# Attention scores of a decoder layer: two heads as two 64-row products instead of one product with block-diagonal keys

## The chip, the cores and the metric

The kernel runs on one core of one Trainium2 chip. The metric is the device time of one execution in microseconds (us); lower is better. All inputs lie in the chip's main memory at the start, and the output is stored there.

## The reference, cut to what matters

The reference is a decoder layer on four sequences of 256 tokens of width 512, with a layer norm after each of three parts. The change touches the second part, attention to 64 context positions with 32 query heads that share 8 key and value heads:

```python
x = _layernorm(x + _L0_attn_ref(x, ...))                  # x @ masked (w1.T w2.T), gelu
x = _layernorm(x + _L0_xattn_ref(x, ctx, ctx, mask, wq, wk, wv, wo, 0))
x = _layernorm(x + _L0_ffn_ref(x, ...))                   # dense + routed low-rank part
# in _L0_xattn_ref:
q = (query @ wq).reshape(bs, sq, HQ, DK).transpose(0, 2, 1, 3)    # HQ = 32, DK = 128, sq = 256
k = (key @ wk).reshape(bs, sk, HKV, DK)                           # HKV = 8, sk = 64
v = (value @ wv).reshape(bs, sk, HKV, DV)
...                                                               # each k, v head serves 4 query heads
q = apply_rope(q, pos)
k = apply_rope(k, ...)
scores = jnp.einsum('bhqd,bhkd->bhqk', q, k) / scale
attn = jax.nn.softmax(scores + m[:, None, :, :], axis=-1)
out = jnp.einsum('bhqk,bhkd->bhqd', attn, v)
return out.transpose(0, 2, 1, 3).reshape(bs, sq, HQ * DV) @ wo
```

## The kernel before, in words

The 1024 tokens are 8 tiles (`t`) of 128, two tiles to a sequence. Attention goes in 8 groups (`g`), one for each key/value head, with its 4 query heads. Groups 1 to 6 are a hardware loop (`Fori(1, LAST)`, `LAST` is 7); group 0 and group 7 are written out around it. Nothing is scheduled while it runs: every engine has its own list of steps in an order written out by hand, and the engines keep step by counting semaphores (`wait_ge`). An engine never passes a step that waits.

Most large products are made of three products of a rounded 32-bit type, high and low parts, by `mm3` (L255 to L257): the high part times the high part, and the two mixed ones. ScalarE (ACT) makes the high part by a copy (L763), and VectorE (DVE) or GpSimd (POOL) the low part by a subtraction (L1102 on VectorE). The steps of one group on TensorE (PE) are:

- `keys(g)`, `values(g)`: keys and values of the group's head.
- `query(g, u, f)`, 8 times: queries of a unit. A unit `u` (4 in a group, `UNITS`) is two heads (`a` = 0, 1) times 512 tokens. `f` is 0 or 1 for the first or second 64 of the 128 dimensions of a head, as the rotary embedding pairs them. So in `QR[:, u % 2, f, tokens]` the partitions 0 to 63 hold dimensions of one head and 64 to 127 the same dimensions of the other.
- `scores(g, u)` (L348): plain 32-bit products. For each of 4 token tiles and both `f` the stationary operand is `QR` (128 partitions by 128 tokens) and the moving one is `KBD`, 128 by 128, the keys written block-diagonally: head 0's 64 rows go with columns 0 to 63, head 1's with columns 64 to 127, and zeros stand elsewhere. So one product gives both heads' scores. One such product in 32 bits is two weight loads and two matmul instructions in the trace.
- VectorE then takes the scores in PSUM (`mask_scores` L1241, `row_max` L1246, `shift` L1253), ScalarE does the exponential (L860), VectorE the sums and inverses (L1258, L1262), GpSimd the scaling (`probs`, L1697).
- `probs_transpose(g, u)` (L355): the probabilities transposed, 4 tiles.
- `value_out(g, n, b)`: values times the output weights, 3 matmuls into bank `b`; high and low parts go to `VWh` and `VWl`.
- `attend(g, t)`: probabilities times `VW`, 6 matmuls; `accumulate` (L1280) adds the bank to the residual `X`.

The 8 PSUM banks are given out by hand: 0 and 1 for queries with `f` = 0, 2 for `f` = 1, 3 for `value_out`, 4 for scores, 5 for transposed probabilities, 6 and 7 for `attend` in turn. Behind group 7 each tile's statistics are taken on VectorE, GpSimd finds the inverse root by Newton steps (L1676 to L1682), ScalarE normalizes, and `x2_tile(t)` (L261) transposes the tile for the dense part (`base`, `lora_in`, `lora_out`). The product at L300, with one row (`PTh[0:1, ...]`), adds the bias in the first dense part, once in each of 8 tiles; L386, L421 and L426 are small products of the router.

Of the kernel before, what the change touches and what calls it, by code (L numbers as in the profile page):

```python
# [15 lines left out]
P = 128  # L16
# [15 lines left out]
def decoder_layer(nc, x, ctx_in, amask, w1, w2, b2, smask, wq, wk, wv, wo, fW, fb, fA, fB, rW, rb, rope, out):  # L32
# [24 lines left out]
    with ExitStack() as es:  # L57
# [18 lines left out]
        KBD = sb("KBD", [P, B, 2, P])  # L76
# [31 lines left out]
        QB_BANK, S_BANK, T_BANK, PV_BANK = 2, 4, 5, 6  # L108
# [4 lines left out]
        kbd_zero wq_hi wq_lo wo_hi wo_lo wkv_hi wkv_lo k_mm k_sw k_cos k_sin k_add k_rot v_mm v_hi v_lo  # L113
# [38 lines left out]
        def v_out(g):  # L152
            return bank[:, T_BANK if isinstance(g, int) and g == 0 else 1, 0:B * KS]
# [4 lines left out]
        def x2_bank(t):  # L158
            return (3, 5, 4, 4, 5, 3, 5, 3)[t]
# [14 lines left out]
        def by_head(ap, t):  # L174

            return ap.rearrange("p (a t k) -> p a t k", a=2, k=KS)[:, :, t, :]

        def fy_bank(t):
            return (0, 6, 2, 7, 1, 3, 2, 7)[t]
# [8 lines left out]
        F_BANKS = (1, 3, 3, 2, 2, 1, 1)  # L188
        LORA_BANKS, ROUTE_BANK = (4, 3), 5
# [62 lines left out]
        def _(pe):  # L252
# [87 lines left out]
            def scores(g, u):  # L340
# [26 lines left out]
            def attend(g, t):  # L367
# [5 lines left out]
                for pair in range(2):  # L373
                    m = mm3(bank[:, PV_BANK + t % 2, :], PTh[:, pair, t * P:(t + 1) * P], PTl[:, pair, t * P:(t + 1) * P],
# [114 lines left out]
            pe.wait_ge(sm["x_added"], 8)  # L489
            value_out(0, 0, 3)  # L490
# [4 lines left out]
            pe.wait_ge(sm["tr_lo"], 14)  # L495
# [3 lines left out]
            pe.wait_ge(sm["vw_lo"], n_vw(0, 0))  # L499
# [5 lines left out]
            pe.wait_ge(sm["vw_lo"], n_vw(0, 1))  # L505
            value_out(0, 2, 3)
            pe.wait_ge(sm["k_cos"], 1)
            scores(0, 0)
            pe.wait_ge(sm["q_rot"], n_rot(0, 0, 0))
            query(0, 2, 0)  # L510
            pe.wait_ge(sm["vw_lo"], n_vw(0, 2))
# [7 lines left out]
            pe.wait_ge(sm["v_lo"], 1)  # L519
# [3 lines left out]
            pe.wait_ge(sm["vw_lo"], n_vw(0, 3))  # L523
            value_out(0, 4, 3)
# [7 lines left out]
            value_out(0, 5, 3)  # L532
            pe.wait_ge(sm["tr_lo"], 17)
            attend(0, 0)
# [1329 lines left out]
```

## Time and profile before

| | before |
|---|---|
| median of 3 runs | 520.07 us (520.02 to 523.38) |
| the profiled execution, its own time | 519.7 us |
| its span on the core | 517.9 us |
| outside the span | 1.8 us |
| mean granted TensorE clock | 0.992 of full |
| TensorE matmul busy | 498.5 us, 96% of the span |
| TensorE weight load busy | 420.7 us |
| VectorE, ScalarE, GpSimd busy | 411.5, 259.6, 268.0 us |

The span is from the first to the last instruction that the profile shows. A matmul's row has the start at which it was taken up and a modelled end, so neighbours overlap; what a matmul costs in a stream is the distance from its start to the start of the next.

### The profile page before, as it was taken

The page shows a single profiled execution, that of the slowest core. Times are in us where ns is not written, and L with a number is a line of the kernel's source. Part 1 is how long each engine was busy: PE and PEld are TensorE (multiplying, and loading weights), DVE is VectorE, ACT ScalarE, POOL GpSimd, SP SyncE. Part 2 cuts the span into 40 slices and gives each one's busy share as a digit, 9 for nine tenths or more (in the row PEclk, how much of TensorE's full clock was granted, in tenths as well). Part 3 has the DMA queues.
Part 4 walks back from the last instruction along what each step waited for, and adds up shares of the span by engine and source line. Part 5 has one row for each costly group of instructions (what it writes and reads, how often), then busy time and mean ns, then how long its engine had stood idle before and what let it go on. Part 6 is the DMA issues. An engine that isn't in the chain of part 4 may idle for free.

```text
span 517.9 us, 7997 instructions
## 1 busy us (share of the span) xinstructions
PE 498.5 (96%) x2637; PEld 420.7 (81%) x2637; DVE 411.5 (79%) x742; ACT 259.6 (50%) x462; POOL 268.0 (52%) x344
## 2 busy tenths in 40 slices
PE   5999999999999999999999999999999999989992
PEld 4777788888888888888888888888888888868781
DVE  4557789887888778878887888788878869999475
ACT  4372375763465355635653574367346635363332
POOL 3173264873575358436742675276627632127724
PEclk9999999999999999999999999999999999989998
DMA  8942010122013002300230023002200230000004
GB/s 296 356 139 106 1 41 1 56 76 74 1 53 132 18 0 81 121 0 0 81 121 0 0 81 121 0 0 81 81 0 0 93 51 1 1 1 1 1 0 163
DMA packets 27596, 31.48 MB, mean 61 GB/s; under 512 B 6321, under 2 KB 14769, under 8 KB 27578
## 3 DMA queue, kind: packets, MB, share of 16 engines
q1 hardware_dynamic: 27578, 31.25, 18.9%
q8 instruction: 10, 0.16, 0.1%
q14 instruction: 8, 0.07, 0.0%
HBM read 29.15 MB, written 2.10 MB: 60 GB/s over the span
## 4 chain that ended last, share of the span: by engine, by line
PE 90%; DVE 2%; POOL 2%; DMA 2%; issue 1%; SPq 1%; ACT 1%; POOLq 0%; DVEq 0%
PE bank L255 24%; PE bank L257 24%; PE bank L256 24%; PE bank L348 11%; PE bank L355 3%; PE bank L261 2%; DMA CTX<-in_ctx_dram 2%; PE bank L300 1%; PE bank L388 1%; DVE VWl L1102 1%; POOL NW L1680 1%; POOL NW L1678 0%; POOL RS L1682 0%; POOL NW L1676 0%; DVE BST L1152 0%
## 5 line engine op out<-in xcount | busy, mean ns | idle before, releaser
L1691 POOL TENSOR_TENSOR QS<-QS,SIN 128x512 f32<-128x512 f32 x64 | 83.0, 1296 | 131.8 <-ACT QS L763 126.7
L1102 DVE TENSOR_TENSOR VWl<-bank,VWh 64x512 fp32r<-64x512 f32 (+1 forms) x132 | 90.9, 689 | 21.3 <-ACT VWh L763 19.4
L255 PE MATMUL bank<-XTh,WQh 128*128 128x512 f32 x256 | 102.3, 400 | 0.0
L763 ACT ACTIVATE VWh<-bank 64x512 fp32r<-64x512 f32 (+1 forms) x132 | 78.1, 592 | 45.4 <-PE bank L257 43.1
L257 PE MATMUL bank<-XTh,WQl 128*128 128x512 f32 x256 | 99.9, 390 | 0.0
L256 PE MATMUL bank<-XTl,WQh 128*128 128x512 f32 x256 | 99.8, 390 | 0.0
L763 ACT ACTIVATE QS<-bank 128x512 f32<-128x512 f32 x64 | 38.3, 599 | 112.7 <-PE bank L257 112.6
L348 PEld LDWEIGHTS bank<-KBD,QR 128*128 128x128 f32 x512 | 61.8, 191 | 2.3
L348 PE MATMUL bank<-KBD,QR 128*128 128x128 f32 x512 | 62.3, 275 | 0.0
L1216 DVE TENSOR_TENSOR bank<-bank,COS 128x512 f32<-128x512 f32 x64 | 44.6, 697 | 20.2 <-ACT QS L763 19.8
L1667 POOL TENSOR_TENSOR WOl<-WOr,WOh 128x512 fp32r<-128x512 f32 x32 | 41.1, 1288 | 31.9 <-ACT WOh L763 31.9
L257 PEld LDWEIGHTS bank<-XTh,WQl 128*128 128x128 f32 x256 | 48.0, 188 | 10.3
L256 PEld LDWEIGHTS bank<-XTl,WQh 128*128 128x128 f32 x256 | 48.2, 188 | 9.2
L255 PEld LDWEIGHTS bank<-XTh,WQh 128*128 128x128 f32 x256 | 48.2, 188 | 9.1
L255 PE MATMUL bank<-VWh,PTh 128*128 128x512 f32 x128 | 51.2, 400 | 0.0
L257 PE MATMUL bank<-VWh,PTl 128*128 128x512 f32 x128 | 50.1, 391 | 0.0
L256 PE MATMUL bank<-VWl,PTh 128*128 128x512 f32 x128 | 49.9, 390 | 0.0
L1226 DVE TENSOR_TENSOR QR<-bank,QS 128x512 f32<-128x512 f32 x64 | 43.2, 680 | 2.3 <-POOL QS L1691 2.1
L1280 DVE TENSOR_TENSOR X<-X,bank 128x512 f32<-128x512 f32 x64 | 42.8, 677 | 1.2 <-PE bank L257 0.6
L1657 POOL TENSOR_TENSOR WQl<-WQr,WQh 128x512 fp32r<-128x512 f32 x32 | 41.2, 1300 | 3.0 <-ACT WQh L763 3.0
L1697 POOL TENSOR_TENSOR SM<-SM,RI 128x512 f32<-128x512 f32 x32 | 33.5, 1048 | 13.2 <-DVE RI L1262 13.1
L255 PE MATMUL bank<-WOh,VTh 128*128 128x512 f32 x64 | 27.3, 427 | 2.3 <-DVE VWl L1102 2.2
(146 smaller groups left out, 953.7 us busy)
## 6 DMA issues: line engine op xcount, KB each, us to landing
WQr<-in_L_xattn_wq_dram SPq DMA_DIRECT2D x8, 1024.0 KB, 5.5
WOr<-in_L_xattn_wo_dram SPq DMA_DIRECT2D x8, 1024.0 KB, 5.4
KVr<-in_L_xattn_wk_dram SPq DMA_DIRECT2D x8, 256.0 KB, 3.8
KVr<-in_L_xattn_wv_dram SPq DMA_DIRECT2D x8, 256.0 KB, 4.1
out_dram<-X SPq DMA_DIRECT2D x8, 256.0 KB, 2.1
X<-in_x_dram SPq DMA_DIRECT2D x3, 512.0 KB, 9.4
WQr<-in_L_attn_w_dram SPq DMA_DIRECT2D x4, 256.0 KB, 3.4
WOr<-in_L_attn_w_dram SPq DMA_DIRECT2D x4, 256.0 KB, 4.8
```

Of the source, the lines that this page charges most:

```text
L255: pe.matmul(o, lh, rh, start=start, stop=False)
L256: pe.matmul(o, lh, rl, start=False, stop=False)
L257: return pe.matmul(o, ll, rh, start=False, stop=stop)
L348: m = pe.matmul(by_head(bank[:, S_BANK, :], t), QR[:, u % 2, f, t * P:(t + 1) * P], KBD[:, b, f, :].rearrange("p (a k) -> p a k", a=2), st ...
L763: return act.activation(o, i, ACT.Copy)
L1102: return dve.tensor_tensor(o, i, f32(hi), ALU.subtract)
L1216: dve.tensor_tensor(q, q, by_pos(COS, 2, S), ALU.mult).then_inc(sm["q_cos"], 1)
L1226: dve.tensor_tensor(QR[:, u % 2, f, :], bank[:, q_bank(u, f), :], QS[:, u % 2, 1 - f, :], ALU.add if f else ALU.subtract).then_inc(sm["q_r ...
L1280: dve.tensor_tensor(X[:, t, :], X[:, t, :], bank[:, PV_BANK + t % 2, :], ALU.add)\
L1657: pool.tensor_tensor(wq_split(WQl, h), wq_head(WQr, h), f32(wq_split(WQh, h)), ALU.subtract)\
L1667: pool.tensor_tensor(WOl[:, h, :], WOr[:, h, :], f32(WOh[:, h, :]), ALU.subtract)\
L1691: pool.tensor_tensor(q, q, SIN[:, :].unsqueeze(1).broadcast_to([P, 2, S]), ALU.mult)\
```

## The change: what it does

The keys are no longer written block-diagonally. `KK` holds them densely: partitions 0 to 63 and 64 to 127 each have the same 64 dimensions, 64 keys wide. `scores` issues, for each token tile and each `f`, two products of 64 rows: head 0's on partitions 0 to 63 and head 1's on 64 to 127, each 128 tokens stationary and 64 keys moving, into the same columns of two different PSUM banks (4 and 5). The 8 products of a unit become 16. Nothing is written in zeros any more (the memset on GpSimd and its semaphore are gone).

Since scores now hold two banks, the other banks are given out anew: transposed probabilities go to bank 7 or 5 by unit, `attend` to 7, 3, 7, 6, 3, 7, 6, 7 by tile, and `value_out` to 3, 6 or 7. The written-out orders of all four engines are other ones, with other waits; VectorE's and ScalarE's operations on scores have the same sizes over two banks.

```diff
-        KBD = sb("KBD", [P, B, 2, P])
+        KK = sb("KK", [P, B, 2, KS])
...
-        QB_BANK, S_BANK, T_BANK, PV_BANK = 2, 4, 5, 6
+        QB_BANK, S_BANK, PV_BANK = 2, 4, 6
+        T_BANKS, A_BANKS = (7, 7, 5, 7), (7, 3, 7, 6, 3, 7, 6, 7)
...
+        def s_all():
+            return bank[:, S_BANK:S_BANK + 2, 0:4 * KS]
...
                 for t in range(4):
                     b = 2 * (u // 2) + t // TPB
                     for f in range(2):
-                        m = pe.matmul(by_head(bank[:, S_BANK, :], t), QR[:, u % 2, f, t * P:(t + 1) * P],
-                                      KBD[:, b, f, :].rearrange("p (a k) -> p a k", a=2), start=f == 0, stop=f == 1)
+                        for a in range(2):
+                            head = slice(64 * a, 64 * a + 64)
+                            m = pe.matmul(bank[:, S_BANK + a, t * KS:(t + 1) * KS], QR[head, u % 2, f, t * P:(t + 1) * P],
+                                          KK[head, b, f, :], start=f == 0, stop=f == 1)
                 m.then_inc(sm["s_mm"], 1)
...
-                    m = pe.transpose(bank[:, T_BANK, t * P:(t + 1) * P], SM[:, u % 2, t * P:(t + 1) * P], ID[:, :])
+                    m = pe.transpose(bank[:, T_BANKS[u], t * P:(t + 1) * P], SM[:, u % 2, t * P:(t + 1) * P], ID[:, :])
...
-                    m = mm3(bank[:, PV_BANK + t % 2, :], PTh[:, pair, t * P:(t + 1) * P], PTl[:, pair, t * P:(t + 1) * P],
+                    m = mm3(bank[:, A_BANKS[t], :], PTh[:, pair, t * P:(t + 1) * P], PTl[:, pair, t * P:(t + 1) * P],
...
-                        m = copy(KBD[64 * a:64 * a + 64, :, f, KS * a:KS * a + KS],
+                        m = copy(KK[64 * a:64 * a + 64, :, f, :],
                                  KC[64 * f:64 * f + 64, :].rearrange("p (b k) -> p b k", b=B))
...
-            pool.memset(KBD[:, :, :, :], 0.0).then_inc(sm["kbd_zero"], 1)
```

The orders are shown at three places. The first is TensorE in the loop, around the scores of a unit 0: what stands there before.

```order
L255 MATMUL bank<-WOh,VTh 128x512 [waits v_lo,wo_lo]
L256 MATMUL bank<-WOl,VTh 128x512
L257 MATMUL bank<-WOh,VTl 128x512
L559 REGISTER_ALU
L342 ISA [waits s_sub]
L348 MATMUL bank<-KBD,QR 128x2x64 [waits k_rot,q_rot]
L348 MATMUL bank<-KBD,QR 128x2x64 x7
L330 REGISTER_ALU [waits v_lo]
L255 MATMUL bank<-XTh,WQh 128x512 [waits wq_lo]
```

And the same place in the changed kernel:

```order
L257 MATMUL bank<-XTh,WQl 128x512
L342 ISA [waits pt_lo,s_sub]
L350 MATMUL bank<-KK,QR 128x64 [waits k_rot,q_rot]
L350 MATMUL bank<-KK,QR 128x64 x15
L255 MATMUL bank<-WOh,VTh 128x512 [waits wo_lo,vw_lo]
L256 MATMUL bank<-WOl,VTh 128x512
```

8 products stand as 16, half as wide; the scores also wait for `pt_lo`, since their second bank, 5, is the one of unit 2's transposed probabilities; and the query of unit 1 stands ahead of them instead of behind.

The second place is TensorE behind group 7's scores: the last `value_out` steps (`WOh,VTh`), the last `probs_transpose` (`ID,SM`) and the first `x2_tile` (`ID,X`). Before:

```order
L255 MATMUL bank<-WOh,VTh 128x512 [waits vw_lo]
L256 MATMUL bank<-WOl,VTh 128x512
L257 MATMUL bank<-WOh,VTl 128x512
L355 MATMUL bank<-ID,SM 128x128 [waits p_done,pt_lo]
L355 MATMUL bank<-ID,SM 128x128 x3
L255 MATMUL bank<-WOh,VTh 128x512 [waits vw_lo]
L256 MATMUL bank<-WOl,VTh 128x512
L257 MATMUL bank<-WOh,VTl 128x512
L388 MATMUL bank<-ID,WOr 128x128 [waits fa_in,f_lo]
```

In the changed kernel:

```order
L390 MATMUL bank<-ID,WQr 128x128 [waits q_rot]
L390 MATMUL bank<-ID,WQr 128x128 x3
L357 MATMUL bank<-ID,SM 128x128 [waits p_done,x_added]
L357 MATMUL bank<-ID,SM 128x128 x3
L255 MATMUL bank<-VWh,PTh 128x512 [waits vw_lo]
...
L261 MATMUL bank<-ID,X 128x128 [waits ln_out,s_sub]
L261 MATMUL bank<-ID,X 128x128 x3
L261 MATMUL bank<-ID,X 128x128 [waits ln_out,pt_lo]
L261 MATMUL bank<-ID,X 128x128 x3
```

One `attend` (6 matmuls) stands now between the last `probs_transpose` and the first `x2_tile`; before, one `value_out`, two weight transposes and three `attend` did.

The third place is GpSimd's start. Before:

```order
L1735 MEMSET KSW 1x128
L1736 MEMSET KBD 128x1024
L1715 TENSOR_TENSOR WOl<-WOr,WOh 128x512 x2
L1662 TENSOR_TENSOR KVl<-KVr,KVh 128x512 x2
L1657 TENSOR_TENSOR WQl<-WQr,WQh 128x4x2x64 x2
```

In the changed kernel:

```order
L1736 ISA
L1736 AFFINE_SELECT ID<-ID 128x128
L1738 MEMSET KSW 1x128
L1718 TENSOR_TENSOR WOl<-WOr,WOh 128x512 x2
L1665 TENSOR_TENSOR KVl<-KVr,KVh 128x512 x2
```

One memset is gone, and nothing else moved there.

## Rows read from the trace of the kernel before

**Rows 1.** The page: busy time, and the chain that ended last, by engine and line.

```profile
PE 498.5 (96%) x2637; PEld 420.7 (81%) x2637; DVE 411.5 (79%) x742; ACT 259.6 (50%) x462; POOL 268.0 (52%) x344
...
PE bank L255 24%; PE bank L257 24%; PE bank L256 24%; PE bank L348 11%; PE bank L355 3%; PE bank L261 2%; DMA CTX<-in_ctx_dram 2%; PE bank L300 1%; PE bank L388 1%; DVE VWl L1102 1%; POOL NW L1680 1%; POOL NW L1678 0%; POOL RS L1682 0%; POOL NW L1676 0%; DVE BST L1152 0%
```

**Rows 2.** Busy time of each engine by stretch: one loop pass, and behind the last scores.

```profile
core 0: us, PE busy (x) PEld busy (x) DVE busy (x) ACT busy (x) POOL busy (x), PEclk, DMA share, GB/s
...
176.00:226.00 50.00, 50.00 (x273) 43.13 (x273) 41.18 (x67) 26.38 (x49) 28.23 (x24) 1.00 0.17 52
...
445.00:484.00 39.00, 35.90 (x179) 28.67 (x177) 34.30 (x76) 18.04 (x30) 17.87 (x62) 0.96 0.00 1
```

**Rows 3.** TensorE groups of the scores: 512 matmuls, and their 512 weight loads.

```profile
L348 PE MATMUL bank<-KBD,QR 128*128 128x128 f32 x512 | 62.3, 275 | 0.0
...
L348 PEld LDWEIGHTS bank<-KBD,QR 128*128 128x128 f32 x512 | 61.8, 191 | 2.3
```

**Rows 4.** TensorE in time (start, us): a score unit with transposes behind it.

```profile
204.93 0.39 PE L257 MATMUL bank<-XTh,WQl 128*128 128x512 f32 x1
205.16 1.95 PE L348 MATMUL bank<-KBD,QR 128*128 128x128 f32 x16
206.94 0.60 PE L355 MATMUL bank<-ID,SM 128*128 128x128 f32 x4
```

**Rows 5.** TensorE's weight loads in time, right behind them.

```profile
207.27 0.19 PEld L255 LDWEIGHTS bank<-WOh,VTh 128*128 128x128 f32 x1
207.38 0.19 PEld L256 LDWEIGHTS bank<-WOl,VTh 128*128 128x128 f32 x1
```

**Rows 6.** Matmuls in time around two products of one row, L300 and L301.

```profile
43.42 0.39 PE L257 MATMUL bank<-VWh,XTl 128*128 128x512 f32 x1
43.74 0.49 PE L300 MATMUL bank<-PTh 1*128 1x512 f32 x1
44.07 0.39 PE L301 MATMUL bank<-PTl,PTh 1*128 1x512 f32 x1
44.40 0.50 PE L255 MATMUL bank<-VWh,XTh 128*128 128x512 f32 x1
44.73 0.40 PE L256 MATMUL bank<-VWl,XTh 128*128 128x512 f32 x1
```

**Rows 7.** Weight loads at the same place.

```profile
43.74 0.18 PEld L300 LDWEIGHTS bank<-PTh 1*128 1x128 f32 x1 [0.35 <-issue]
43.84 0.18 PEld L301 LDWEIGHTS bank<-PTl,PTh 1*128 1x128 f32 x1
44.39 0.19 PEld L255 LDWEIGHTS bank<-VWh,XTh 128*128 128x128 f32 x1 [0.36 <-issue]
```

**Rows 8.** Matmuls in time around the router's 8 products with 4 stationary columns.

```profile
488.43 0.35 PE L421 MATMUL bank<-RWT,QT 128*4 128x8 f32 x8
488.71 0.50 PE L255 MATMUL bank<-XTh,WOh 128*128 128x512 f32 x1
```

**Rows 9.** TensorE in time behind the last scores: first and last of each wait.

```profile
455.15 0.40 PE L257 MATMUL bank<-WOh,VTl 128*128 128x512 f32 x1
457.16 0.50 PE L255 MATMUL bank<-WOh,VTh 128*128 128x512 f32 x1 [1.61 <-DVE VWl L1102]
...
459.13 0.79 PE L255 MATMUL bank<-WOh,VTh 128*128 128x512 f32 x1 [0.57 <-DVE VWl L1102]
459.72 0.63 PE L256 MATMUL bank<-WOl,VTh 128*128 128x512 f32 x1
460.15 0.63 PE L257 MATMUL bank<-WOh,VTl 128*128 128x512 f32 x1
460.58 1.78 PE L388 MATMUL bank<-ID,WOr 128*128 128x128 f32 x8
```

**Rows 10.** GpSimd in time at the start.

```profile
1.55 0.94 POOL L1736 MEMSET KBD<- 128x1024 f32 x1
8.88 1.28 POOL L1715 TENSOR_TENSOR WOl<-WOr,WOh 128x512 fp32r<-128x512 f32 x1 [6.39 <-ACT WOh L763]
```

More of the change, by code:

```diff
@@ L152, in v_out @@
         def v_out(g):
-            return bank[:, T_BANK if isinstance(g, int) and g == 0 else 1, 0:B * KS]
+            return bank[:, 5 if isinstance(g, int) and g == 0 else 1, 0:B * KS]
         def tr_bank(n):
@@ L590, in _ @@
                 query(g, 3, 0)
+                pe.wait_ge(sm["x_added"], n_added(g - 1, 7))
+                probs_transpose(g, 0)
+                pe.wait_ge(sm["x_added"], n_added(g - 1, 6))
+                value_out(g, 4, 6)
                 pe.wait_ge(sm["q_rot"], n_rot(g, 2, 0))
                 keys(g + 1)
+                pe.wait_ge(sm["q_rot"], n_rot(g, 2, 1))
+                query(g, 3, 1)
+                pe.wait_ge(sm["s_sub"], n_unit(g, 1))
+                scores(g, 2)
                 pe.wait_ge(sm["pt_lo"], n_unit(g, 0))
@@ L622, in _ @@
+            value_out(LAST - 1, 7, 3)
+            pe.wait_ge(sm["x_added"], n_added(LAST - 1, 0))
+            attend(LAST - 1, 2)
+            pe.wait_ge(sm["vw_lo"], n_vw(LAST - 1, 5))
+            attend(LAST - 1, 3)
+            pe.wait_ge(sm["s_sub"], n_unit(LAST - 1, 3))
+            probs_transpose(LAST - 1, 2)
             pe.wait_ge(sm["v_lo"], LAST + 1)
             query(LAST, 1, 0)
+            pe.wait_ge(sm["s_sub"], n_unit(LAST - 1, 3))
             pe.wait_ge(sm["pt_lo"], n_unit(LAST - 1, 2))
+            scores(LAST, 0)
@@ L637, in _ @@
             query(LAST, 2, 0)
[L638 to L641 removed]
+            pe.wait_ge(sm["pt_lo"], n_unit(LAST - 1, 3))
+            value_out(LAST, 1, 7)
+            pe.wait_ge(sm["vw_lo"], n_vw(LAST, 0))
+            attend(LAST - 1, 4)
+            pe.wait_ge(sm["s_sub"], n_unit(LAST, 0))
+            scores(LAST, 1)
             pe.wait_ge(sm["q_rot"], n_rot(LAST, 1, 1))
@@ L651, in _ @@
-            query(LAST, 3, 0)
-            pe.wait_ge(sm["vw_lo"], n_vw(LAST, 0))
-            weight_transpose(1)
+            pe.wait_ge(sm["q_rot"], n_rot(LAST, 2, 0))
+            weight_transpose(0)
+            pe.wait_ge(sm["x_added"], n_added(LAST - 1, 4))
+            value_out(LAST, 3, 3)
+            pe.wait_ge(sm["q_rot"], n_rot(LAST, 2, 1))
+            query(LAST, 3, 1)
+            pe.wait_ge(sm["pt_lo"], n_unit(LAST, 0))
+            attend(LAST - 1, 5)
+            pe.wait_ge(sm["vw_lo"], n_vw(LAST, 2))
@@ L694, in _ @@
+            probs_transpose(LAST, 3)
+            pe.wait_ge(sm["vw_lo"], n_vw(LAST, 7))
+            attend(LAST, 3)
+            pe.wait_ge(sm["s_sub"], n_unit(LAST, 3))
+            x2_tile(0)
+            pe.wait_ge(sm["pt_lo"], n_unit(LAST, 2))
+            x2_tile(1)
+            pe.wait_ge(sm["vw_lo"], n_vw(LAST, 6))
+            attend(LAST, 4)
+            pe.wait_ge(sm["pt_lo"], n_unit(LAST, 3))
+            attend(LAST, 5)
+            pe.wait_ge(sm["f_lo"], 1)
+            base(0)
             pe.wait_ge(sm["f_lo"], 4)
@@ L840, in k_spread @@
                 act.wait_ge(sm["k_add"], g + 1)
-                if isinstance(g, int) and g == 0:
-                    act.wait_ge(sm["kbd_zero"], 1)
-                else:
+                if not (isinstance(g, int) and g == 0):
                     act.wait_ge(sm["s_mm"], n_unit(g - 1, 3))
@@ L965, in _ @@
             k_swap(0)
[L966 removed]
+            vw_hi(0, 0, 7)
             wkv_hi(1)
@@ L1232, in s_rows @@
             def s_rows():
-                return bank[:, S_BANK, :].rearrange("p (r k) -> p r k", k=KS)
+                return s_all().rearrange("p a (t k) -> p a t k", k=KS)
             def mask_scores(g, u):
```

550 lines of the change are left out of this document (254 added, 296 removed).

## The prediction

> **What bounds the kernel now.** I read the page first, then the busy time by stretch, then TensorE in time. The chain that ended last is nine tenths TensorE, and the score products alone, L348, are 11% of it [rows 1]. In a loop pass TensorE is busy 50.00 of 50.00 us while VectorE, the next engine, is busy 41.18 [rows 2]. Of the 32 units of scores (8 groups times 4; the 512 matmuls are 32 times 16) 24 lie in the six passes and the others right around them. There every microsecond added to or taken from TensorE's work goes straight into the time, and nothing else does, as long as VectorE keeps its 8.8 us of slack. The new order can gain only behind the last scores, where TensorE waits.
>
> **What a unit of scores costs now.** The 16 matmuls of one unit start at 205.16, and what follows starts at 206.94: 1.78 us, 0.111 us for each pair of a weight load and a matmul [rows 4]. Thirty-two of them are 57 us, which is the 11%. The group rows give 275 ns for a matmul and 191 ns for a load [rows 3]; these overlap, so the spacing is the cost, not the duration. Which of the two sets the 0.111? The loads alone can be seen where long matmuls follow: the load at 207.27 is followed by the next at 207.38, 0.11 us later, although the matmul between them is 512 wide [rows 5]. So a load of 128 columns takes 0.11 us of the load path. The matmul has about the same length, or less, hidden behind it. Does a load of fewer rows cost less? The only loads of this kind with fewer rows are those with one row: 43.74 and 43.84, 0.10 us apart [rows 7]. Against 128 rows that is the same. Products of 64 rows lie between one and 128 rows, so I take 0.11 us for each of their loads.
>
> **The change, part by part.**
>
> Score products: a unit's 8 products of 128 rows and 128 moving columns become 16 of 64 rows and 64 columns. Each is still two loads and two matmuls, so 16 loads of 0.11 us become 32. The stationary side, 128 tokens, is as wide as before; only the moving side is halved. The matmul shrinks, at most 0.111 to an estimated 0.055 us by its columns, but the matmul hid behind the load anyway. What decides is whether head 0's loads (rows 0 to 63) and head 1's (rows 64 to 127) go side by side. No row of this trace shows two row halves at work, so I bound it. If they do not overlap, 32 loads are 3.52 us. If they do, the order of the program is A, A, B, B, A, A, B, B (A for head 0, two parts each); a head's next load can start when its last matmul has, the first step holds one load of A alone, and from then on each step of 0.11 us holds one of either head: 17 steps, 1.87 us. I take the second, since the two products share neither rows nor PSUM bank, and price the first as a rival.
>
> The Trainium skill ("TensorEngine Tiling (Array Packing)", Key Properties) says that different tiles can execute weight loads and matmuls in parallel. No run shown here tells; without it the choice stands on the disjoint rows alone.
>
> Changing the shape of the array: the trace shows what a product that doesn't use all the rows costs beside its own work. L300 and L301 use one row. From the matmul at 43.42 to the one at 44.73 are four steps, 1.31 us, where four steps of 0.23 (204.93 to 205.16 [rows 4]) would be 0.92: 0.39 us for going in and coming out [rows 6]. The loads tell why: the one at 43.74 and the one at 44.39 each come after an idle time of 0.35 us and are not pulled ahead of the matmul before them [rows 7]. The same shows at 488.43 to 488.71 with 4 columns: eight pairs in 0.28 us, where the next matmul comes late too [rows 8]. So each way costs 0.09 us until the first load may start (0.32 less 0.23), and then the load itself, 0.11, bare. A unit of 64-row products stands between full-height ones on both sides, so it pays this 32 times in and 32 times out. Bounds: nothing, if half the rows are no other shape, and 0.39 us as here. I take the upper, the only one that a row shows.
>
> The sum for one unit: 0.09 in, 17 steps of 0.11 = 1.87, the last matmul 0.055, 0.09 out, and 0.11 for the next load in the open: 2.22 us, against 1.78. That is 0.44 more, times 32 = **+14 us**.
>
> The Trainium skill (the same page and section) says that changing the tiling mode drains TensorE, and names no price; the trace agrees, with the 0.09 us each way.
>
> Keys: ScalarE's four copies have the same 64x256 size and only land elsewhere; zero. GpSimd's memset, 0.94 us, ends at 2.49 us, and GpSimd then idles 6.39 us for ScalarE [rows 10]: zero, and if that cover were gone, 0.94. VectorE's three operations on scores read two banks instead of one, with the same 512 elements in a row; zero for TensorE, because of the 8.8 us of slack.
>
> New banks and orders in the loop: the same steps, with other waits. New is that scores of unit 0 wait for unit 2's transposed probabilities, whose bank they need; behind that wait stand in TensorE's queue a `value_out` and the next query. A query stands ahead of them now, 12 matmuls of 0.23 us or 2.7 us, which covers the copy and the subtraction. TensorE waits nowhere in the loop before, so nothing can be gained (below: none); a wait of some tenths a pass would give at most 1 us times 8. I take zero, since a slower TensorE leaves all the others more time.
>
> Behind the last scores: TensorE waits 1.61 and 0.57 us for `VWl`, and then takes steps of 0.43 us (459.72 to 460.15) and eight transposes in 1.78 us, where four took 0.60 [rows 4, 9]: its clock is at the lower of its two levels, 1.2 instead of 2.4 GHz, and the granted clock of the whole stretch is 0.96 [rows 2]. The two waits are 2.2 us, the slow spell about one more (0.20 us for each of the three steps, less for the transposes). VectorE, 34.3 of 39 us busy [rows 2], would let a better order return no more than 4.7. The new order takes away the bank shared by neighbours in `value_out`, but puts `x2_tile(0)` a single `attend` behind the last transposes, where three `attend` steps covered the Newton steps on GpSimd. That exposes up to 4.1 us, three times 6 matmuls of 0.23. From -5 to +4; I take zero, the middle.
>
> So 519.7 (span 517.9 and 1.8 around it) plus 14 is 533.7 us. The profiled execution is 0.4 us below the median of 520.07, too little to correct for: **533.6 us**, 2.6% slower.
>
> **Rivals.**
>
> *The halves really run as half-priced work.* If a 64-row load isn't held to 0.11 us but to half of it, a step costs 0.055 us: 0.09 + 17 x 0.055 + 0.055 + 0.09 + 0.11 = 1.28 us, 0.50 less than now, times 32 = -16: **504 us**. It decides as soon as a step of both heads takes less than 0.084 us, where the unit is back at 1.78. For it: the eight pairs of 4 columns follow each other in 0.28 us with the change of shape [rows 8], so instructions as such are no limit, and total multiply work per unit halves. Against it: the one-row loads at 0.10 us [rows 7].
> The Trainium skill ("TensorEngine Tiling (Array Packing)", Theoretical Speedup) gives up to 2x for a small dimension of 64 or less; that is this rival.
>
> *The loads of the two halves do not overlap.* 0.09 + 32 x 0.11 + 0.055 + 0.09 + 0.11 = 3.87 us, 2.09 more, times 32 = +67: **586 us**. For it: all loads of this trace follow one another, and one row holds the path as long as 128 do [rows 5, 7]. Against it: only the lack of a shared row.
>
> *No change of shape is paid, the rest as forecast.* 17 steps of 0.11 are 1.87 us, or 16 if the first hides: between 0 and +0.09, times 32 = 0 to +3: **521 us**. For it: the price was seen with one row and with 4 columns, not with 64 rows. Against it: both show it, in each of the 8 tiles and in the router.
>
> **How the numbers follow.** Forecast as above 44%, half-priced loads 26%, no overlap 16%, no change of shape 14%. The forecast's own range is 525 (no more than half of the change of shape paid, or the whole gain at the end) to 541 (the waits behind the last scores and some in the loop). The range must leave out no more than 2 in 10: with the half-priced case and the free change of shape it is 502 to 541, and only the 16% of 586 lie outside. A measurement of this kernel tells about 1% from no change. Faster by over 1% is the half-priced case and a little more, 0.27; within 1% the free change of shape, 0.13; slower the other two, 0.60.
>
> **What would show it.** In the changed profile the score line should have 1024 matmuls and 1024 loads. Right: a unit takes 2.2 us from its first matmul to the next work, each head's loads are 0.11 us apart and those of both heads interleave, and the loads on both sides of a unit show an idle time of some 0.35 us. The loop pass grows by four units' 0.44, 1.8 us, and TensorE stays busy throughout. A unit of 3.9 us says no overlap, one of 1.3 us says cheap loads. Wrong in another way it would be if the loop showed waits of TensorE for VectorE (`QR`, `VWl` or `PTl`), or if the time behind the last scores moved by more than 5 us.

## The result, and the profile of the changed kernel

| | before | changed |
|---|---|---|
| median | 520.88 us (4 runs, 520.02 to 523.38) | 532.62 us (4 runs, 531.31 to 534.03) |
| span of the profiled execution | 517.9 us | 530.2 us |
| mean granted TensorE clock | 0.992 | 0.994 |

The ratio is 1.0225, with a 95% interval of 1.0199 to 1.025: 11.7 us slower. The forecast was 533.6 us. The total is right to 1 us; two of its terms are not, and they cancel in part.

First the page of the changed kernel, the lines that answer to [rows 1]: busy time, and the chain that ended last.

```profile
PE 507.9 (96%) x3149; PEld 419.4 (79%) x3149; DVE 408.9 (77%) x742; ACT 259.8 (49%) x462; POOL 269.0 (51%) x343
...
PE bank L255 25%; PE bank L257 24%; PE bank L256 24%; PE bank L350 11%; PE bank L357 3%; PE bank L261 2%; DMA CTX<-in_ctx_dram 2%; DVE VWl L1105 1%; PE bank L300 1%; DVE BST L1155 1%; DVE X L1347 1%; PE bank L390 0%; PE bank L301 0%; ACT VW
```

The chain is the same: nine tenths TensorE, the scores (now L350) 11% of the span. 512 more matmuls make TensorE 9.4 us busier. Next the stretches that answer to [rows 2]: a loop pass, now 51.46 us from a step to the same step of the next pass (50.07 before), and 39 us from about the last scores on (in this kernel they start at 458.45).

```profile
core 0: us, PE busy (x) PEld busy (x) DVE busy (x) ACT busy (x) POOL busy (x), PEclk, DMA share, GB/s
180.00:231.50 51.50, 51.50 (x338) 43.15 (x337) 40.96 (x68) 26.50 (x49) 28.56 (x25) 1.00 0.15 51
457.00:496.00 39.00, 34.11 (x197) 27.40 (x195) 34.74 (x77) 19.00 (x31) 18.60 (x63) 1.00 0.00 1
```

In the loop TensorE still never waits, and VectorE's slack grew from 8.8 to 10.5 us. Now the groups of the scores, by form, which answer to [rows 3]:

```profile
L350 PE MATMUL bank<-KK,QR 64*128 64x64 f32 x1024 | 64.1, 275 | 0.0
...
L350 PEld LDWEIGHTS bank<-KK,QR 64*128 64x128 f32 x1024 | 59.6, 188 | 10.9 <-issue 10.8 <-DVE SM L1256 0.2
```

The durations of one (275 and 188 ns) hardly moved against [rows 3], and twice as many instructions keep the engine busy for about as long as before, 64.1 against 62.3 us: they lie on top of each other. The idle time of the loads in front of the scores has grown from 2.3 to 10.9 us, 0.34 us for each of 32 units. Matmuls in time, a unit with transposes behind it, as in [rows 4]:

```profile
198.59 0.39 PE L257 MATMUL bank<-XTh,WQl 128*128 128x512 f32 x1
198.91 2.00 PE L350 MATMUL bank<-KK,QR 64*128 64x64 f32 x32
200.84 0.66 PE L357 MATMUL bank<-ID,SM 128*128 128x128 f32 x4
201.25 0.48 PE L255 MATMUL bank<-WOh,VTh 128*128 128x512 f32 x1
```

And the first six weight loads of that unit, in a narrow window of the timeline, which answer to [rows 5, 7]:

```profile
198.37 0.19 PEld L257 LDWEIGHTS bank<-XTh,WQl 128*128 128x128 f32 x1
198.91 0.41 PEld L350 LDWEIGHTS bank<-KK,QR 64*128 64x128 f32 x6 [0.35 <-issue]
```

Read these two as follows. Six loads span 0.41 us: one load's 0.19 and two steps of 0.11. So they come in three pairs, one load of each head side by side. By the single starts of the matmuls the two of a pair are 6 to 7 ns apart and the pairs 0.112 us, the first step 0.154: 16 pairs, 1.73 us from first to last matmul. On the way in, the matmul of 198.59 is followed after 0.32 us instead of 0.23, with the load idle 0.35 us and not pulled ahead. On the way out the last pair is at 200.64, the next work at 200.84, 0.20 us later. Behind a unit the first load is in the open, so where 512 wide products follow their first step takes 0.34 instead of 0.23 us. The sum: 0.09 + 1.73 + 0.20 + 0.11 = 2.13 us a unit. By the same count a unit before is 0 + 1.67 + 0.03 + 0.09 = 1.79. That is 0.34 more, times 32 = 11.0 us. Both have 16 loads, or pairs of loads, one behind the other, and none of the 0.34 is a load more: 0.09 is on the way in, 0.06 in the first steps, 0.17 on the way out, 0.02 behind.

The stretch behind the last scores answers to [rows 9]: each place where TensorE waits.

```profile
458.45 2.00 PE L350 MATMUL bank<-KK,QR 64*128 64x64 f32 x32
461.24 0.47 PE L255 MATMUL bank<-VWh,PTh 128*128 128x512 f32 x1 [0.78 <-DVE PTl L1105]
...
467.48 0.40 PE L257 MATMUL bank<-WOh,VTl 128*128 128x512 f32 x1
469.45 0.50 PE L255 MATMUL bank<-WOh,VTh 128*128 128x512 f32 x1 [1.57 <-DVE VWl L1105]
```

With the wait of 2.4 us below, these are 4.8 us. The old order showed 2.2 in the stretch of [rows 9], and one more wait further on, at 484.18, which the new order doesn't have: the first line below is of the kernel before. So it is 4.8 against 3.2 us. The other lines are all of the changed kernel's waiting, by what TensorE waited for:

```profile
PE bank L261 <- ACT X L889: 1.0, 1, 1.0
```

```profile
PE bank L255 <- DVE VWl L1105: 4.0, 2, 2.4
PE bank L269 <- DMA WQr<-in_L_attn_w_dram: 3.7, 1, 3.7
PE bank L261 <- DMA CTX<-in_ctx_dram: 1.7, 1, 1.7
PE bank L255 <- DVE WQl L1105: 1.6, 1, 1.6
PE bank L255 <- DVE PTl L1105: 0.8, 1, 0.8
```

GpSimd's start, as in [rows 10]: without the memset it idles 7.35 us for the same copy of ScalarE, so the memset had cost nothing.

```profile
1.42 0.20 POOL L1738 MEMSET KSW<- 1x128 f32 x1
8.96 2.96 POOL L1718 TENSOR_TENSOR WOl<-WOr,WOh 128x512 fp32r<-128x512 f32 x2 [7.35 <-ACT WOh L768]
```

### The profile page after: what moved, and what is told of

The parts are those of the page before. It is cut to its first block, busy times and chain, and to the rows that moved or that the text cites. A ratio compares the mean times of both kernels' runs of the same rounds, so it can differ in the third digit from the quotient of the medians.

```text
span 530.2 us, 9033 instructions
## 1 busy us (share of the span) xinstructions
PE 507.9 (96%) x3149; PEld 419.4 (79%) x3149; DVE 408.9 (77%) x742; ACT 259.8 (49%) x462; POOL 269.0 (51%) x343
## 4 chain that ended last, share of the span: by engine, by line
PE 90%; DVE 3%; DMA 2%; POOL 1%; SPq 1%; issue 1%; ACT 1%; DVEq 0%; POOLq 0%; ACTq 0%
PE bank L255 25%; PE bank L257 24%; PE bank L256 24%; PE bank L350 11%; PE bank L357 3%; PE bank L261 2%; DMA CTX<-in_ctx_dram 2%; DVE VWl L1105 1%; PE bank L300 1%; DVE BST L1155 1%; DVE X L1347 1%; PE bank L390 0%; PE bank L301 0%; ACT VWh L768 0%; SPq L203 0%
## 5 line engine op out<-in xcount | busy, mean ns | idle before, releaser
L350 PEld LDWEIGHTS bank<-KK,QR 64*128 64x128 f32 x1024 | 59.6, 188 | 10.9 <-issue 10.8
L350 PE MATMUL bank<-KK,QR 64*128 64x64 f32 x1024 | 64.1, 275 | 0.0
L1244 DVE SCALAR_TENSOR_TENSOR bank<-bank,MSK 128x512 f32<-128x512 f32 x32 | 22.2, 694 | 15.3 <-PE bank L350 15.3
```

The lines of the kernel that those rows point to most:

```text
L350: m = pe.matmul(bank[:, S_BANK + a, t * KS:(t + 1) * KS], QR[head, u % 2, f, t * P:(t + 1) * P], KK[head, b, f, :], start=f == 0, stop=f == 1)
```

## The experiments

My theory after the result: the time is the row tiles themselves (a step is held to 0.11 us by the 128 columns of its weight load, and a change of shape is paid on both sides of each unit). The rival: the new orders and banks cost it. "One run" means that the kernel was timed once, beside the kernel before on the same chip. The table has the inner times of a typical unit, from the single starts in each trace (ns): the step into the first matmul, first to last, the step out, and the step behind that, between products of 512 columns. Without a unit there would be two steps of 227 in all, so a unit costs the sum of its four numbers less 454.

| kernel | median, us | before, same chip | in | first to last | out | next |
|---|---|---|---|---|---|---|
| before | 520.88 | | 228 | 1670 | 31 | 315 |
| changed | 532.62 | 520.88 | 318 | 1730 | 202 | 338 |
| blockdiag_new_order | 523.17 | 521.39 | as before | | | |
| same_half | 627.76 | 521.39 | 318 | 3510 | 202 | 338 |
| head_outermost | 600.76 | 521.39 | 318 | 3117 | 202 | 335 |
| full_height_between | 550.18 | 521.39 | 318 | 837 + 620 + 837 | 202 | 335 |
| before_half_moving | 522.31 | 522.34 | 228 | 1617 | 84 | 317 |
| before_half_stationary | 530.89 | 522.34 | 318 | 1688 | 202 | 337 |
| before_half_both | 504.89 | 522.34 | 318 | 923 | 152 | 338 |
| one_head | 534.55 | 522.34 | 318 | 1723 | 202 | 338 |
| before_third_bank | 523.54 | 520.50 | as before | | | |
| half_keys | 531.03 | 520.50 | 318 | 1702 | 202 | 338 |
| four_tiles | 516.24 | 521.48 | 318 | 1195 | 148 | 338 |
| four_tiles_throughout | 508.16 | 521.44 | 318 | 943 | 148 | 338 |

**blockdiag_new_order**: the changed kernel's orders and banks, with the old product.

```diff
-                        for a in range(2):
-                            head = slice(64 * a, 64 * a + 64)
-                            m = pe.matmul(bank[:, S_BANK + a, t * KS:(t + 1) * KS], QR[head, u % 2, f, t * P:(t + 1) * P],
-                                          KK[head, b, f, :], start=f == 0, stop=f == 1)
+                        m = pe.matmul(bank[:, S_BANK, :].rearrange("p (a t k) -> p a t k", a=2, k=KS)[:, :, t, :],
+                                      QR[:, u % 2, f, t * P:(t + 1) * P],
+                                      KBD[:, b, f, :].rearrange("p (a k) -> p a k", a=2), start=f == 0, stop=f == 1)
```

> The changed kernel with all its new orders, banks and waits, but the scores as one product of 128 rows with block-diagonal keys again (one bank, the memset too). Theory A, the 64-row products cost it all (0.35 us a unit for the changes of the array's shape, 32 units, 11 us): about 521 us, the time of the kernel before within 1%. Theory B, the new orders and banks cost most of it: 528 us or more.

Measured 523.17 us, ratio to before 1.0033 (1.0018 to 1.0048): 1.8 us slower. A unit is the old one again (197.11 to 198.89, 1.78 us):

```profile
197.11 1.95 PE L348 MATMUL bank<-KBD,QR 128*128 128x128 f32 x16
198.89 0.60 PE L356 MATMUL bank<-ID,SM 128*128 128x128 f32 x4
```

and TensorE's waits are those of the changed kernel:

```profile
PE bank L255 <- DVE VWl L1106: 4.0, 2, 2.4
...
PE bank L255 <- DVE PTl L1106: 0.6, 1, 0.6
```

So of the 2.25% the new orders make about 0.3% and the tiles the remaining 1.9%, some 10 us. The rival has a small share of the truth. That share lies outside the loop: a pass is 50.10 us here, against 50.07 before and 51.46 with the tiles.

**same_half**: both products on rows 0 to 63.

```diff
-                            m = pe.matmul(bank[:, S_BANK + a, t * KS:(t + 1) * KS], QR[head, u % 2, f, t * P:(t + 1) * P],
-                                          KK[head, b, f, :], start=f == 0, stop=f == 1)
+                            m = pe.matmul(bank[:, S_BANK + a, t * KS:(t + 1) * KS], QR[0:64, u % 2, f, t * P:(t + 1) * P],
+                                          KK[0:64, b, f, :], start=f == 0, stop=f == 1)
```

> The changed kernel, but both products of a pair use rows 0 to 63 (head 1's scores are then head 0's: the computation is changed). Theory A, weight loads go side by side only because the heads lie in different halves of the rows: 32 loads in a row instead of 16 pairs, 16 more steps of 0.112 us in each of 32 units, 57 us more, about 589 us. Rival, 64-row loads are quick in any place and the pairs need no second half: 533 us. In a unit: 3.9 us against 2.1.

Measured 627.76 us (one run), where 589 was expected. 32 single steps of 0.11 us are 3.51 us, as the no-overlap arithmetic has it; that much is +57 us over the changed kernel. The other 39 us (by the spans, 625.9 and 530.2) go with the clock: by the mean granted clocks, 0.927 and 0.994, some 90 us of this execution went at half clock and 6 of the changed kernel's, and half of the difference is an estimated 42 us. From the trace, a unit and what follows it, and the row of a window behind it, with the columns of [rows 2]:

```profile
257.68 3.95 PE L349 MATMUL bank<-KK,QR 64*128 64x64 f32 x32
261.57 0.79 PE L255 MATMUL bank<-WOh,VTh 128*128 128x512 f32 x1
262.16 0.63 PE L256 MATMUL bank<-WOl,VTh 128*128 128x512 f32 x1
262.59 0.63 PE L257 MATMUL bank<-WOh,VTl 128*128 128x512 f32 x1
```

```profile
261.50:264.50 3.00, 3.00 (x8) 2.35 (x8) 0.72 (x2) 1.18 (x2) 0.00 (x0) 0.50 1.00 357
```

The full-height products behind that unit go at 0.43 us a step (262.16 to 262.59) instead of 0.23, and the granted clock is 0.50: TensorE is at 1.2 GHz, though it has not idled. 11 of the 32 units end at the lower clock, and the mean granted clock is 0.927.

**head_outermost**: the same products, all eight of head 0 first, then those of head 1.

```diff
-                for t in range(4):
-                    b = 2 * (u // 2) + t // TPB
-                    for f in range(2):
-                        for a in range(2):
-                            head = slice(64 * a, 64 * a + 64)
+                for a in range(2):
+                    head = slice(64 * a, 64 * a + 64)
+                    for t in range(4):
+                        b = 2 * (u // 2) + t // TPB
+                        for f in range(2):
```

> The changed kernel with the same 16 products of a unit in another order: all 8 of head 0, then all 8 of head 1. If TensorE only pairs products that stand close together, nearly all loads follow one another: up to 57 us more, 589 us. If it looks far enough ahead in its queue (14 products), the pairs come together all the same: 533 us. I expect the first, with a few loads hidden: 575 to 590.

Measured 600.76 us (one run), clock 0.950. The unit between 222.26 and 225.58:

```profile
222.26 3.39 PE L350 MATMUL bank<-KK,QR 64*128 64x64 f32 x32
225.58 0.66 PE L357 MATMUL bank<-ID,SM 128*128 128x128 f32 x4
```

By the single starts, head 1's first matmul comes at 223.657, 6 ns behind head 0's 13th of 16; so the last three or four steps are shared (3.51 less 3.12 is 0.39, three and a half steps). Two row tiles that stand far apart in the program hardly meet: what makes the overlap is that `a` is the innermost loop. By the steps alone (3.12 less 1.73, times 32) this is 44 us above the changed kernel, 577 us and within what was expected; the other 24 us go with the lower clock, for which the expectation had no term.

**full_height_between**: a full-height product behind `t` = 1, that is in the middle of each unit (its output goes to columns of bank 4 that nobody reads).

```diff
+                    if t == 1:
+                        pe.matmul(bank[:, S_BANK, 4 * KS:6 * KS], QR[:, u % 2, 0, 0:P], ID[:, :], start=True, stop=True)
```

> The changed kernel with one product of 128 rows and 128 columns put into the middle of every unit, into a part of bank 4 that nobody reads (2 loads, 2 matmuls, 0.22 us as in the kernel before). Theory A, every change of the array's shape costs, a pair of them (out and in) 0.34 us: 0.22 + 0.34 = 0.56 us a unit, times 32 = 18 us, about 550 us. Rival, the 0.35 us are a thing of a unit's start or end, whatever stands there: only 0.22 x 32 = 7 us, about 540 us.

Measured 550.18 us (one run), 17.6 more than the changed kernel, 0.55 us a unit.

```profile
203.85 1.11 PE L350 MATMUL bank<-KK,QR 64*128 64x64 f32 x16
204.89 0.49 PE L353 MATMUL bank<-ID,QR 128*128 128x128 f32 x2
205.31 1.11 PE L350 MATMUL bank<-KK,QR 64*128 64x64 f32 x16
206.34 0.66 PE L359 MATMUL bank<-ID,SM 128*128 128x128 f32 x4
```

The product itself is two steps, 0.22 us; the other 0.33 is going out and in again. That is the price of the change of shape by itself, and the whole of the 0.34 that a unit of the changed kernel costs more. A second pair of changes costs as much as the first.

**before_half_moving, before_half_stationary, before_half_both**: which of load and matmul holds the step of 0.11 us? The kernel before, computing only a part of the scores: half the keys, half the tokens, or both.

The edit of before_half_moving:

```diff
-                        m = pe.matmul(by_head(bank[:, S_BANK, :], t), QR[:, u % 2, f, t * P:(t + 1) * P],
-                                      KBD[:, b, f, :].rearrange("p (a k) -> p a k", a=2), start=f == 0, stop=f == 1)
+                        m = pe.matmul(by_head(bank[:, S_BANK, :], t)[:, :, 0:32], QR[:, u % 2, f, t * P:(t + 1) * P],
+                                      KBD[:, b, f, :].rearrange("p (a k) -> p a k", a=2)[:, :, 0:32], start=f == 0, stop=f == 1)
```

> The kernel before, with only 32 of the 64 keys of each head moving in the score products (64 moving columns instead of 128; the other scores are left out). Theory A, the weight load of 128 columns sets the step of 0.112 us: the step stays, the unit stays 1.79 us, the time stays 520 us. Rival, the matmul sets it: the step falls towards 0.056 us, 0.9 us a unit, 29 us less, 491 us.

That of before_half_stationary; before_half_both has both edits.

```diff
-                        m = pe.matmul(by_head(bank[:, S_BANK, :], t), QR[:, u % 2, f, t * P:(t + 1) * P],
+                        m = pe.matmul(by_head(bank[0:64, S_BANK, :], t), QR[:, u % 2, f, t * P:t * P + 64],
```

> The kernel before, with only 64 of the 128 tokens of each tile stationary (loads of 64 columns; the scores of the other tokens are left out), all 128 columns moving. If the matmul of 128 moving columns takes as long as a load (my estimate from the spacing of the transposes, 0.109 us, whose loads are shorter), the step stays 0.11 us; with the change of shape to 64 columns, 0.3 us a unit, about 530 us. If the load alone set the step, it would fall to 0.06 us: about 505 us.

> The kernel before, with 64 tokens stationary and 64 columns moving (a quarter of the scores is computed). Both the load and the matmul are halved: a step of 0.056 to 0.06 us, 16 steps in 0.9 us, and 0.3 us for the change of shape: 0.55 us a unit less, 18 us, about 502 us, by every theory that has load and matmul as the limits. If something else held the step (issue of instructions), it would stay at 0.11 us and the time at 530 us.

One run each: 522.31, 530.89 and 504.89 us, beside 522.34 for the kernel before. First the group of before_half_moving's score matmuls, whose mean and sum hardly differ from [rows 3] (its steps are in the table); then, in time, a unit of before_half_stationary and one of before_half_both:

```profile
L348 PE MATMUL bank<-KBD,QR 128*128 128x64 f32 x512 | 60.6, 271 | 0.0
```

```profile
210.42 1.96 PE L348 MATMUL bank<-KBD,QR 128*64 128x128 f32 x16
212.31 0.66 PE L355 MATMUL bank<-ID,SM 128*128 128x128 f32 x4
```

```profile
200.43 1.15 PE L348 MATMUL bank<-KBD,QR 128*64 128x64 f32 x16
201.51 0.66 PE L355 MATMUL bank<-ID,SM 128*128 128x128 f32 x4
```

Halving the matmul alone changes nothing, since the load holds 0.11; halving the load alone neither, since the matmul of 128 columns holds 0.11 too; both halved give 0.058 a step. The step is the longer of the two, and each goes by its own columns. before_half_stationary is even 8.6 us slower: a stationary side of 64 columns is also another shape, and pays the way in and out. The changed kernel halves the moving side only, so its steps had to stay at 0.11.

**one_head**: the changed kernel without head 1's products (its scores are left out).

```diff
-                        for a in range(2):
+                        for a in range(1):
```

> The changed kernel with the products of head 0 alone (head 1's bank keeps what stood there: its scores are left out). Theory A, the second half of the rows costs nothing beside the first: the same 16 steps of 0.112 us, the same 2.13 us a unit, 532 us. Rival, head 1's products add their own time in part: less than 530 us. If lone 64-row products pull TensorE's clock down, as the granted clock of 0.93 with all products in one half suggests, it shows here too, with a granted clock below 0.99 and more than 532 us.

Measured 534.55 us (one run, clock 0.984). A unit:

```profile
200.46 2.00 PE L350 MATMUL bank<-KK,QR 64*128 64x64 f32 x16
202.39 0.66 PE L357 MATMUL bank<-ID,SM 128*128 128x128 f32 x4
```

Half the instructions take as long as all of them: 1.93 us from the first matmul to the transposes, as in the changed kernel. The second half of the array works at no cost. The mean granted clock is 0.984 against 0.994. The expectation asked whether lone 64-row products pull the clock down here too. Three windows of this trace, with the columns of [rows 2], say that they don't:

```profile
0.00:79.00 79.00, 71.10 (x329) 55.45 (x329) 47.80 (x104) 36.88 (x66) 31.79 (x63) 0.96 0.47 154
180.00:231.43 51.43, 51.43 (x274) 43.08 (x273) 40.91 (x67) 26.44 (x48) 28.48 (x24) 1.00 0.16 51
475.00:490.00 15.00, 14.91 (x69) 12.42 (x70) 13.20 (x34) 5.82 (x9) 7.35 (x26) 0.89 0.01 2
```

The lower clock lies ahead of the first scores and behind the last ones; in a loop pass it is 1.00, and a pass takes 51.43 us, as in the changed kernel. The 1.9 us above that kernel are within what one run can't tell: its own four runs go from 531.31 to 534.03.

**half_keys**: the changed kernel with 32 of 64 keys moving (the other scores are left out).

```diff
-                                          KK[head, b, f, :], start=f == 0, stop=f == 1)
+                                          KK[head, b, f, 0:32], start=f == 0, stop=f == 1)
```

> The changed kernel with 32 of the 64 keys moving in each 64-row product (the other scores are left out). The load of 128 columns sets the step of each head's stream: still 0.112 us, a unit of 2.13 us less some 0.03 for the last matmul, 532 us. If the matmuls of two heads shared something that made the step, it would fall below 0.112 us and the time below 530.

Measured 531.03 us (one run), 1.6 less than the changed kernel; from first to last are 1.70 us instead of 1.73, so the steps stay at 0.11: the loads hold them, as before_half_moving says.

**before_third_bank**: can the old order do better behind the last scores, where I had put up to 4.7 us? The kernel before, whose `value_out(7, 6)` and `(7, 7)` get banks 3 and 7, so that the last does not wait for its neighbour's bank.

```diff
-            pe.wait_ge(sm["vw_lo"], n_vw(LAST, 4))
-            value_out(LAST, 6, 7)
+            pe.wait_ge(sm["f_lo"], 3)
+            value_out(LAST, 6, 3)
...
-            pe.wait_ge(sm["vw_lo"], n_vw(LAST, 5))
-            value_out(LAST, 7, 6)
+            pe.wait_ge(sm["vw_lo"], n_vw(LAST, 4))
+            value_out(LAST, 7, 7)
...
-            pe.wait_ge(sm["vw_lo"], n_vw(LAST, 6))
+            pe.wait_ge(sm["vw_lo"], n_vw(LAST, 7))
```

> The kernel before, with block-diagonal keys and its own orders, but behind the last scores value_out(7, 6) goes to bank 3 instead of 7 and value_out(7, 7) to bank 7 instead of 6, so that TensorE need not wait there for VectorE to empty a bank just filled (waits of 1.61 and 0.57 us, and then a slow spell). If those waits are a matter of banks: 2 to 4 us less than before, ratio 0.992 to 0.996. If VectorE, 34.3 of 39 us busy there, is the bound, TensorE waits later instead: within 1 us of before.

Measured 523.54 us, ratio 1.0054 (1.0035 to 1.0073): 3 us slower, which neither side of the expectation had.

```profile
459.85 1.03 PE L388 MATMUL bank<-ID,WOr 128*128 128x128 f32 x8
465.53 0.80 PE L255 MATMUL bank<-VWh,PTh 128*128 128x512 f32 x1 [4.65 <-DVE VWl L1102]
466.12 0.63 PE L256 MATMUL bank<-VWl,PTh 128*128 128x512 f32 x1
466.55 0.63 PE L257 MATMUL bank<-VWh,PTl 128*128 128x512 f32 x1
```

```profile
465.50:470.50 5.00, 4.97 (x12) 3.91 (x13) 1.97 (x4) 0.00 (x0) 0.00 (x0) 0.50 0.01 3
```

The first wait, 1.61 us [rows 9], is gone, and a later one of 4.65 us has come: TensorE waits 5.1 us for `VWl` instead of 2.2. `value_out(7, 7)` now stands in the bank that `attend(7, 3)` needs, so this waits for the last of VectorE's subtractions instead of the one before. In the window of the second fence (the columns are those of [rows 2]) the granted clock is 0.50 for 5 us, and twelve matmuls go at 0.43 us. So the gain that I had bounded by 4.7 us wasn't to be had by moving these banks; whether another order gets it was not tried.

**four_tiles**: what the half-size runs point to is a load of half the columns. The changed kernel with each product split once more by tokens, so that the array is four tiles of 64 by 64; only the first product of each head in a unit stays 128 wide. Nothing is left out.

```diff
-                            m = pe.matmul(bank[:, S_BANK + a, t * KS:(t + 1) * KS], QR[head, u % 2, f, t * P:(t + 1) * P],
-                                          KK[head, b, f, :], start=f == 0, stop=f == 1)
+                            w = P if t == 0 and f == 0 else 64
+                            for c in range(0, P, w):
+                                m = pe.matmul(bank[c:c + w, S_BANK + a, t * KS:(t + 1) * KS],
+                                              QR[head, u % 2, f, t * P + c:t * P + c + w],
+                                              KK[head, b, f, :], start=f == 0, stop=f == 1)
```

> The changed kernel, and each product of 64 rows by 128 tokens is split once more into two of 64 tokens (columns 0 to 63 and 64 to 127 of the array), except the first product of each head in a unit, which stays 128 tokens wide. Nothing is left out. In the changed kernel a unit costs 2.13 us (0.09 in, 1.73 from first to last start, 0.20 out, 0.11 load), and loads and matmuls half as wide follow each other at 0.058 us where both are halved. Theory A, the load path is held by the columns of one tile and all four tiles go side by side: 0.15 + 0.11 + 14 steps of 0.058 = 1.08 us from first to last, unit 1.48, 0.65 less than now, times 32 = -21, about 512 us; with one more change of shape (0.2 us) between the 128 wide product and the rest, 518. Theory B, the two column halves of one row half share the load path: 28 steps of 0.058 in place of 14 of 0.112, first to last 1.9 us, about +0.16 a unit, 538 us. Theory C, tiles of 64 columns lower the granted clock or pay their own changes: slower than 545.

Measured 516.24 us, ratio to before 0.9914 (0.9881 to 0.9946). It lies between the two prices of theory A, 512 and 518. Its first to last is 1.195 us against the 1.08 of theory A: the four tiles step together every 58 ns, and between the 128 wide pair and them lies 0.208 us, another change of shape.

**four_tiles_throughout**: that pair split like the rest, with the unit's waits on an empty instruction of their own.

```diff
+                pe.nop(nofuse=True)
...
+                            for hh in range(2):
+                                head, half = slice(64 * a, 64 * a + 64), slice(64 * hh, 64 * hh + 64)
+                                m = pe.matmul(bank[half, S_BANK + a, t * KS:(t + 1) * KS],
+                                              QR[head, u % 2, f, t * P + 64 * hh:t * P + 64 * hh + 64],
+                                              KK[head, b, f, :], start=f == 0, stop=f == 1)
```

> four_tiles with the first product of each unit cut in four tiles like the others, so that a unit has one shape. Its waits stand on an instruction of their own ahead of the first load. Nothing is left out. In four_tiles a unit takes 1.195 us from first to last start: 0.154 and 0.208 for the two steps of the 128 wide pair, 0.833 for the rest. Theory A: the wide pair and the change of shape behind it cost these 0.36 us, and two steps of four tiles would take 0.15 together: 0.21 less a unit, times 32 = -7, about 509 us. Theory B: the separate wait holds back the first load by about what is saved: 514 to 518 us.

Measured 508.16 us, ratio to before 0.9749 (0.9722 to 0.9776), faster than both kernels, and within 1 us of theory A. Matmuls in time, and the first twelve loads of the unit:

```profile
192.96 0.39 PE L257 MATMUL bank<-XTh,WQl 128*128 128x512 f32 x1
193.28 1.16 PE L352 MATMUL bank<-KK,QR 64*64 64x64 f32 x64
194.37 0.66 PE L360 MATMUL bank<-ID,SM 128*128 128x128 f32 x4
```

```profile
193.28 0.27 PEld L352 LDWEIGHTS bank<-KK,QR 64*64 64x64 f32 x12 [0.35 <-issue]
```

64 matmuls, four times those of before, take 1.09 us to the next work, where 16 took 1.78 [rows 4]. Twelve loads span 0.27 us: three groups of four loads each. By the table a unit costs 1.29 us, 0.84 less than in the changed kernel, 27 us over 32; 24.5 arrive. A loop pass shrinks by the full amount, from 51.46 to 48.12 us. The rest, some 2.5 us, is lost outside the loop. TensorE's waits in the two profiled executions come to 13.9 and 11.8 us: 0.5 of the difference is the wait for `PTl`, 1.3 instead of 0.8, and 0.9 the one for the load of `CTX`, 2.6 instead of 1.7. That is most of it; no run separates it further.

## Why the prediction was right, and where it was not

**The bound.** Right. TensorE is busy through the whole loop pass in every variant: no trace has an idle time of it there, and each microsecond of a unit is seen 32 times.

**Loads of the two halves overlap, at 0.11 us a step.** Right, and it is the step on which the total hung. The pairs are 6 to 7 ns apart and same_half shows the other world, 3.51 us a unit. The Trainium skill ("TensorEngine Tiling (Array Packing)", Key Properties) says that different tiles can load and multiply in parallel; the trace agrees. head_outermost adds a condition that the section does not have: they do so only when they stand close together in the program.

**17 steps, and a last matmul of 0.055.** Wrong, and the mis-sized term. I let the first step hold one load of head 0 alone, but both heads start together, so it is 16 pairs. The last pair starts 1.73 us behind the first (15 steps, of which the first takes 0.154), where 17 steps would put it at 1.76; and from there to the next work I had 0.11 + 0.055 + 0.09 = 0.255 us, where the trace has 0.20, with the last matmul inside it. Forecast 2.22 us a unit, measured 2.13; +0.44 became +0.34, 14 us became 11.0.

**The change of shape, paid in full on both sides.** Right. full_height_between gives 0.33 us for one way in and out, and before_half_stationary shows that columns count as shape too. I had it from a product of one row, 0.39 us [rows 6, 7]. The places of the old kernel with other shapes, these and the router's [rows 8], take the same 1.31 and 0.28 us in the changed kernel.

**The orders taken as zero.** Half right. In the loop zero holds. Behind the last scores the new order waits 4.8 us where the old one waited 3.2, though with the clock at 1.00 instead of 0.96 over the 39 us, and blockdiag_new_order puts all of it at 1.8 us. My range of -5 to +4 held it, the middle did not, and nor did the reasons on either side. I had counted on the wait for a bank just filled going away: one of 1.57 us is still there, since `value_out(7, 7)` has bank 6 behind `value_out(7, 5)`. And I had feared an exposed `x2_tile`: it waits nowhere, and the longest wait, 2.41 us, is that of the `attend` ahead of it for `VWl`. The old order's wait of 1.0 us in a later `x2_tile` I had not counted at all. So +14 and 0 came out as +10 to 11 and +1 to 2, and the total came out right partly by cancellation.

**The rival "half-priced work", 504 us.** It had 26% and did not come: it needed a step of 0.055 us, and a load of half the rows doesn't give that; one of half the columns does. With four tiles a unit costs 1.29 us, close to the 1.28 of this rival, and the last run measured 508.16 us. "No overlap" was priced at 586 us from the steps alone; the run of it took 628, since I had no term for the clock. The Trainium skill (the same page, Theoretical Speedup) gives up to 2x for a small dimension of 64 or less. With rows and columns both cut, four_tiles_throughout gave 1.8 times (the same scores in 0.94 instead of 1.67 us from first to last start); for rows alone the change gave none, because the product with block-diagonal keys had already filled all 128 rows and the load's 128 columns stayed.

## What to carry to other kernels

Price a small product by the longer of its load (stationary columns) and its matmul (moving columns), here 0.11 us for 128 columns and 0.058 for 64 of either, and not by how full the array is: cutting rows in two helps only if it frees one of these. A stretch in another tile shape costs a fixed 0.3 us or so at its two ends, so make it long, keep one shape throughout, and put the tiles that should overlap innermost. And measure the orders apart from the instruction change: two effects of different sign or size can give a total that looks explained.

## What the runs showed that I had not expected

- Four tiles load side by side, two of them in the same rows (0.058 us for four loads of 64 columns).
- TensorE's granted clock fell without TensorE idling: units of lone 64-row steps brought the mean granted clock to 0.927 (same_half, 3.5 us from first to last) and 0.950 (head_outermost, 3.1 us). Pairs did not (0.994, 1.73 us), but neither did the lone steps of one_head in its loop (1.72 us), so lone steps alone are not enough; no run has a long unit of pairs, and whether length or the half-empty array counts is not shown.
- Two row tiles 16 matmuls apart in the program overlapped only from the 13th matmul on. From there on, by the spacing of the starts (0.055 us apart instead of 0.11), head 1's matmuls start in between head 0's last three, which stand ahead of them in the program.
- One wait of 4.65 us cost more than itself: the granted clock was 0.50 over the 5 us behind it, where the changed kernel, with waits of 1.57 and 2.41, kept 1.00 over the whole stretch. The longest wait doesn't decide it alone: the clock fell behind waits of 1.61 and 0.57 us in the kernel before [rows 9], and in four_tiles_throughout, whose waits of 1.58 and 2.40 us are nearly those of the changed kernel, it was 0.57 over the 4 us around the end of the second.
